# Running 26 expert tiles inside the attention steps of a fused expert–attention–expert block, and routing the second expert network earlier

## The reference

```
x = x + 0.5 * ffn(layernorm(x))      # "first network"
x = x + attention(layernorm(x))
x = x + 0.5 * ffn(layernorm(x))      # "second network", the same weights
# ffn: scores = softmax(x @ gate.T); the top 2 of 8 experts by scores + bias;
#      every routed row is scaled by its score, then
#      h = silu(row @ w1[e]) * (row @ w3[e]); out = h @ w2[e]   (128 -> 352 -> 128)
# attention: 16 heads of 8, softmax over 256 keys, output projection
```

## Time and profile before

| | |
|---|---|
| time, median of 3 runs | 758.16 us (757.82 to 762.54) |
| span of the profiled execution | 758.1 us, 14824 instructions |
| TensorE busy by its records | 618.2 us, 82% of the span |
| TensorE weight loads | 468.5 us, 62% |
| VectorE busy | 444.4 us, 59% |
| ScalarE busy | 388.9 us, 51% |
| GpSimd busy | 303.9 us, 40% |
| mean granted TensorE clock | 0.943 of full speed |

### The profile page before, as it was taken

How to read it: one execution, slowest core, us unless ns; L and a number is a source line. 1 busy time by engine, 2 the same in 40 slices (tenths; PEclk the granted TensorE clock), 3 DMA queues, 4 the chain that set the end, 5 groups by cost and what they waited for, 6 DMA issues and landing times.

```text
span 758.1 us, 14824 instructions
## 1 busy us (share of the span) xinstructions
PE 618.2 (82%) x5002; PEld 468.5 (62%) x5002; DVE 444.4 (59%) x1163; ACT 388.9 (51%) x910; POOL 303.9 (40%) x313
## 2 busy tenths in 40 slices
PE   5248999999979769899999998885999989999200
PEld 5237998999857334455554554454889979989200
DVE  4845652225346688989999999981567422233111
ACT  0524665444422456777777777773356544444000
POOL 6057533665423255014200010003475137777574
PEclk9999999999999788999999999997999999999755
DMA  7255888887982444345533444016479778887332
GB/s 255 70 182 158 237 237 224 228 239 211 265 262 75 128 130 136 101 133 157 160 101 101 148 127 120 3 44 206 128 194 244 240 191 232 263 236 229 112 80 62
DMA packets 116298, 126.02 MB, mean 166 GB/s; under 512 B 12480, under 2 KB 99008, under 8 KB 115968
## 3 DMA queue, kind: packets, MB, share of 16 engines
q1 hardware_dynamic: 98256, 100.15, 44.2%
q0 software_dynamic: 9088, 18.63, 9.9%
q10 hardware_dynamic: 8880, 6.30, 2.5%
HBM read 89.37 MB, written 35.39 MB: 165 GB/s over the span
## 4 chain that ended last, share of the span: by engine, by line
PE 53%; DVE 23%; DMA 7%; issue 6%; POOL 5%; ACT 4%; SPq 2%; POOLq 0%; ACTq 0%; DVEq 0%
PE banks L677 12%; DVE mx L809 10%; PE banks L649 9%; PE banks L658 8%; PE banks L665 8%; POOL rows L583 4%; PE banks L1061 4%; PE banks L467 2%; PE banks L639 2%; DMA xe<-routed_rows,idx 2%; PE banks L945 2%; PE banks L1034 1%; DMA X<-in_x 1%; DVE resid L796 1%; ACT PT L1075 1%
## 5 line engine op out<-in xcount | busy, mean ns | idle before, releaser
L563 POOL DMA_INDIRECT xe<-routed_rows,idx x156 | 151.4, 971 | 240.4 <-DMA routed_rows<-xn 102.6
L809 DVE TENSOR_REDUCE mx<-banks 128x2 f32<-128x512 f32 x256 | 163.2, 683 | 7.9 <-PE banks L1036 6.6
L1075 ACT ACTIVATE PT<-banks 128x512 f32<-128x512 f32 x256 | 140.6, 604 | 36.7 <-PE banks L1047 34.4
L583 POOL DMA_INDIRECT rows<-slots_out,slot x128 | 124.3, 971 | 71.1 <-issue 28.7
L730 DVE TENSOR_TENSOR hidT<-banks,act 96x256 f32<-96x256 f32 (+1 forms) x92 | 34.9, 380 | 197.2 <-ACT act L711 194.3
L677 PE MATMUL banks<-WR,hidT 128*128 128x128 f32 x936 | 119.8, 275 | 0.6 <-ACT ye L720 0.6
L677 PEld LDWEIGHTS banks<-WR,hidT 128*128 128x128 f32 x936 | 111.9, 191 | 3.0 <-issue 1.0
L649 PE MATMUL banks<-xeT,WR 128*128 128x256 f32 (+1 forms) x368 | 88.8, 365 | 7.6 <-DMA WR<-in_experts 3.4
L658 PE MATMUL banks<-xeT,WR 128*96 128x256 f32 (+1 forms) x368 | 84.7, 353 | 0.3 <-DVE hidT L730 0.3
L665 PE MATMUL banks<-xeT,WR 128*128 128x256 f32 (+1 forms) x368 | 82.8, 347 | 0.0
L1034 PE MATMUL banks<-KS,QS 56*128 56x256 bf16 x256 | 69.1, 286 | 12.2 <-DVE mx L809 10.5
(11 more groups left out here) (158 smaller groups left out, 870.3 us busy)
## 6 DMA issues: line engine op xcount, KB each, us to landing
WR<-in_experts SPq DMA_DIRECT2D x92, 544.0 KB
stacks<-split SPq DMA_DIRECT2D x32, 384.0 KB
slots_out<-ye SPq DMA_DIRECT2D x156, 64.0 KB
QS<-stacks SPq DMA_DIRECT2D x64, 112.0 KB
KS<-stacks SPq DMA_DIRECT2D x64, 112.0 KB
routed_rows<-xn ACTq DMA_DIRECT2D x16, 256.0 KB, 6.1
routed_rows<-xn SPq DMA_DIRECT2D x12, 256.0 KB, 2.3
xe<-routed_rows,idx POOLq DMA_INDIRECT x156, 4.7
```

The source lines that it names most:

```text
L563: eng.indirect_dma_start(xe[:, i % XR, a, :], None, routed_rows[h], bass.IndirectOffsetOnAxis(ap=idx[h][:, tile:tile + 1], axis=0))\
L583: eng.indirect_dma_start(rows[:, k, t, :], None, slots_out[h], bass.IndirectOffsetOnAxis(ap=slot[h][:, k, t:t + 1], axis=0))\
L809: eng.tensor_reduce(mx[:, :, e, pair], maxima_bank(f)[:, :].rearrange("p (q n) -> p q n", q=2), AX.X, ALU.max).then_inc(s_max, 1)
L1075: eng.activation(PT[:, u % 4, 1 - k].rearrange("p t n -> p (t n)"), PS[f % 3], ACT.Exp, scale=scale).then_inc(s_exp2, 1)
```

## The change

Loads 38 to 52 (`I0` to `I1`) leave the expert stages. They are 14 tiles of the first network (38 to 45) and 12 of the second (46 to 52). Each is computed as single tiles inside attention, one tile in two steps, a piece in each half step (`beat`): TensorE's pieces are gate columns, the previous tile's down product, value columns, the next tile's turn. Such a tile uses two banks of its own: `E1` (bank 2) holds gate columns and turned rows, `E2` (bank 7) holds value columns and the result. While they run, scores have banks 0 and 1 and maxima 3 and 4; between steps 17 and 84 (maxima) or 102 (scores) the third bank is back. Silu is taken as 0.5 z (1 + tanh(z / 2)): ScalarE does tanh, VectorE two `scalar_tensor_tensor`.

Attention now begins at step -13 (13 steps ahead of step 0 instead of 8) and holds batch 0's maxima there. The first 14 tiles run from step -13, the other 12 from step 104. Routing g = 2 is moved to steps 58 to 100, right behind batch 7. Half of its rows, and now half of g = 3's, are scaled by VectorE (`rows_vector`). `keep_pace` is gone. Routing g = 3 gets tables of its own counted from load 53, with three ticks of statistics inside attention. SyncE's weight fetches, result stores and row stores are placed in attention by due steps (`joint_due`, `until`). GpSimd's waits follow (`turned`).

The core of the diff, with what the next sections speak of:

```diff
+I0 = NL + 15
+I1 = HALVES * NL + 7
+STEP1 = -13
+STEP2 = 104
+WIDE_FROM = 17
+WIDE_MAX = 84
+WIDE_SCORE = 102
...
+def bank_turns(step_of, two, three, last_wide):
+
+    turns, held = [], {}
+    for f in range(BATCH * HEADS):
+        ring = three if WIDE_FROM <= step_of(f) < last_wide else two
+        bank = min(ring, key=lambda b: held.get(b, -1))
+        turns.append((bank, held.get(bank, -1) + 1))
+        held[bank] = f
+    return turns, held
+
+
+MAXIMA, MAXIMA_END = bank_turns(lambda f: f // 2 + STEP1, (3, 4), (3, 4, 7), WIDE_MAX)
+SCORES, SCORES_END = bank_turns(lambda f: f // 2, (0, 1), (0, 1, 2), WIDE_SCORE)
...
+        def rows_vector(eng, g):
+
+            eng.wait_ge(s_coef, 2 * (g + 1))
             eng.wait_ge(s_comb, GC * HALVES)
+            h = g % HALVES
             for t in range(TH):
-                eng.tensor_scalar(rows[:, 1, t, :], X[:, t, :], factor[:, 1, t:t + 1], offset[:, 1, t:t + 1],
+                if t % 4 == 0:
+                    eng.wait_ge(s_xn[t // 4], 16 * TOP_K * g)
+                eng.tensor_scalar(rows[:, 1, t, :], X[:, h * TH + t, :], factor[:, 1, t:t + 1], offset[:, 1, t:t + 1],
                                   ALU.mult, ALU.add).then_inc(s_xv, 1)
...
+        def rows_sync(eng, g):
+
+            for c in range(RG):
+                if g == 2:
+                    eng.wait_ge(s_xr, rows_made(g) + 4 * c + 4)
                     rows_store(eng, 0, 4 * c + 3, xn)
-                else:
-                    eng.wait_ge(s_xv, 4 * c + 4)
-                    rows_store(eng, 0, TH + 4 * c + 3, rows[:, 1])
+                eng.wait_ge(s_xv, TH * (g - 2) + 4 * c + 4)
...
+        def load_sync(eng, i, first, last):
+
+            if i < last:
+                weights(eng, i)
+            if i >= first + RING:
+                rows_out(eng, i - RING)
...
+        def joint_sync(eng, begin, end, first, last):
+
+            for i in range(begin, end):
+                load_sync(eng, i, first, last)
+                yield
+
+        def joint_due(begin, first, start, early):
+
+            def due(step):
+                n = 0
+                for i in range(begin, I1 + RING):
+                    tile = tiles_before(i - RING + 1) - tiles_before(first)
+                    ready = early if i < first + RING else start + (4 * tile + 2) // 2 + 1
+                    n += ready <= step
+                return n
+            return due
...
+            def turn(i, a, t):
+                if a == 0:
+                    eng.wait_ge(s_xe[i % XR], landed(i))
+                if t == J1:
+                    eng.wait_ge(s_exp2, SCORES_END[2] + 1)
+                wait(eng, s_jgate, t)
+                eng.transpose(E1[:, HC * P:], xe[:, i % XR, a, :], ident).then_inc(s_jxt, 1)
+
+            def up(i, a, t, bank, column):
+                for c in range(HC):
+                    k = P if c < HC - 1 else HT
+                    first = column + c * P
+                    done = eng.matmul(bank[0:k, c * P:(c + 1) * P], WR[:, i % WRING, first:first + k],
+                                      xeT[:, t % 2, 0:P], start=True, stop=True)
+                return done
+
+            def up_gate(i, a, t):
+                if a == 0:
+                    eng.wait_ge(s_wl[i % WRING], 16 * (i // WRING + 1))
+                eng.wait_ge(s_jxte, t + 1)
+                up(i, a, t, E1, 0).then_inc(s_ju1, 1)
+
+            def up_value(i, a, t):
+                if t == 0:
+                    eng.wait_ge(s_ve, 2)
+                if t == J1:
+                    eng.wait_ge(s_lgread, 2 * 3)
+                wait(eng, s_jye, t)
+                up(i, a, t, E2, HIDDEN).then_inc(s_ju3, 1)
+
+            def down(i, a, t):
+                eng.wait_ge(s_jhid, t + 1)
+                for c in range(HC):
+                    k = P if c < HC - 1 else HT
+                    done = eng.matmul(E2[:, HC * P:], hidT[0:k, t % 2, c * P:(c + 1) * P],
+                                      WR[0:k, i % WRING, 2 * HIDDEN + c * D:2 * HIDDEN + (c + 1) * D],
+                                      start=c == 0, stop=c == HC - 1)
+                done.then_inc(s_jy, 1)
+
+            tiles = joint_tiles(first, last)
+            turn(*tiles[0])
+            for j, tile in enumerate(tiles):
+                up_gate(*tile)
+                yield
+                if j > 0:
+                    down(*tiles[j - 1])
+                yield
+                up_value(*tile)
+                yield
+                if j + 1 < len(tiles):
+                    turn(*tiles[j + 1])
+                yield
+            yield
+            down(*tiles[-1])
+            yield
+
...
+            def copy_x(i, a, t):
+                eng.wait_ge(s_jxt, t + 1)
+                wait(eng, s_ju3, t - 1)
+                if t == 0:
+                    eng.wait_ge(s_u3, I0)
+                eng.copy(xeT[:, t % 2, 0:P], E1[:, HC * P:]).then_inc(s_jxte, 1)
+
+            def gate(i, a, t):
+                eng.wait_ge(s_ju1, t + 1)
+                wait(eng, s_jhid, t - 1)
+                if t == 0:
+                    eng.wait_ge(s_hid, I0)
+                eng.activation(act1[:, t % 2, 0:HC * P], E1[:, 0:HC * P], ACT.Tanh, scale=0.5).then_inc(s_jtanh, 1)
+
+            def copy_y(i, a, t):
+                eng.wait_ge(s_jy, t + 1)
+                if a == 0:
+                    wait(eng, s_st[i % RING], stored(i - RING))
+                eng.copy(ye[:, i % RING, a, :], E2[:, HC * P:]).then_inc(s_jye, 1)
...
+            for j, tile in enumerate(tiles):
+                yield
+                gate(*tile)
+                yield
+                if j > 0:
+                    copy_y(*tiles[j - 1])
+                yield
+                yield
+                yield
+                if j + 1 < len(tiles):
+                    copy_x(*tiles[j + 1])
+                yield
+                yield
+                yield
...
+            for i, a, t in joint_tiles(first, last):
+                yield
+                yield
+                eng.wait_ge(s_jtanh, t + 1)
+                eng.scalar_tensor_tensor(act1[:, t % 2, 0:HC * P], act1[:, t % 2, 0:HC * P], 1.0, E1[:, 0:HC * P],
+                                         ALU.add, ALU.mult).then_inc(s_jgate, 1)
+                yield
+                eng.wait_ge(s_ju3, t + 1)
+                eng.wait_ge(s_jgate, t + 1)
+                wait(eng, s_jy, t - 1)
+                if t == 0:
+                    eng.wait_ge(s_y, I0)
+                eng.scalar_tensor_tensor(hidT[:, t % 2, 0:HC * P], act1[:, t % 2, 0:HC * P], 0.5, E2[:, 0:HC * P],
+                                         ALU.mult, ALU.mult).then_inc(s_jhid, 1)
+                yield
+
+        def beat(streams, step):
+
+            for start, stream in streams:
+                if step >= start:
+                    next(stream, None)
...
-        def keep_pace(eng, products):
-
-            for _ in range(products):
-                eng.matmul(PS[4][:, 0:D], ident, WO[:], start=True, stop=True)
+        def steps():
+
+            for step in range(STEP1, PAIRS * BATCH):
+                n, u = divmod(step, PAIRS)
+                yield step, n, u, (2 <= n + 3 < BATCH, 0 <= n + 1 < BATCH, 0 <= n < BATCH, 0 <= n - 1 < BATCH)
...
+                for k in range(2):
+                    largest = largest_scores(eng, maxima_of(n, u), k)
+                    scores = head_scores(eng, n, u, k) if now else iter(())
+                    for _ in range(2):
+                        next(largest, None)
+                        next(scores, None)
...
+                if u % 2 == 0 and u > 0 and now:
+                    values(eng, n, u // 2 - 1)
+                if u == 0 and done:
+                    values(eng, n - 1, PAIRS // 2 - 1)
+                if u == 0 and n >= 2:
+                    turn_raw(eng, n - 2)
+                if ahead and u == 0:
+                    m = n + 3
...
-        def attention_scalar(eng, side, ticks):
...
+        def attention_scalar(eng, streams, side, ticks):
+            for step, n, u, (ahead, nxt, now, done) in steps():
...
+                for k in range(2):
+                    beat(streams, step)
                     if now:
-                        wait(eng, s_av, PAIRS // 2 * n + u // 2 - 1)
-                        for k in range(2):
-                            f = 2 * (PAIRS * n + u) + k
-                            eng.wait_ge(s_sc, f + 1)
-                            eng.activation(PT[:, u % 4, 1 - k].rearrange("p t n -> p (t n)"), PS[f % 3], ACT.Exp,
-                                           scale=scale).then_inc(s_exp2, 1)
...
+        def attention_sync(eng, *sides):
+
+            def until(step, counts):
+                for i, (side, due) in enumerate(sides):
+                    for _ in range(due(step) - counts[i]):
+                        next(side, None)
+                    counts[i] = max(counts[i], due(step))
...
+            for n in range(-2, BATCH):
                 if 2 <= n + 2 < BATCH:
```

(47 more changed lines are left out.)

484 lines of the change are left out of this document (239 added, 245 removed).

## The result

The changed kernel takes **794.33 us** (median of 4 runs, 792.74 to 797.79) against 757.99 beside it: ratio 1.0493 [1.0438, 1.0548], 36 us slower where 19 us faster were forecast. Its profiled execution spans 791.3 us. Times of runs are medians; of e8 and e10 the profiled execution was over 1.5% slower than the fastest of its kernel, and their ratios leave it out. The windows of the changed kernel are cut where the first scores of step 0 (243.5), step 16 (295.0) and step 104 (504.7) start, 0.5 us ahead of the exponentials at which the earlier trace rows cuts steps 16 and 104.

The account below looks back on a forecast made before the run. Attention was taken as bound by VectorE, 94% busy, with about 0.55 us of TensorE free per step. Against 758.1 us, -22.5 + 6.8 + 25 - 26.5 - 2 = -19.2 gave 739 us, range 729 to 750.

Parts of the forecast that it names:

- Part 1: Cost of one joint tile inside attention: 5.55 us per tile, 2.8 a step, with 2.5 as the floor.
- The loop that I drew round VectorE: In full joint steps, the next tile's turn waits for VectorE's first operation, queued behind a maximum: 5.55 us per tile.
- Lockstep: Rival for joint steps: each half step ends on a round trip, 3.5 us a step, +35, 774 us; chance 0.09.
- theory B: Follow-up theory for joint steps: each is a chain of round trips between TensorE, VectorE and ScalarE.
- Parts 2 and 3: Part 2: steps -13 to -1 take 33 us, gain 22.5; Part 3: steps 0 to 15 take 45, loss 6.8.
- Part 4: Routing g = 2 in steps 81 to 100, where nothing hides VectorE's work: +25 us (19 to 30).
- Part 5: Step 104 to load 53: 64 us (56 to 75) instead of 90.3, a gain of 26.5.
- Part 6: From load 53 on: 2 us gained (-3 to +3) from load 69's wait; last gathers unchanged.

Follow-up runs that it names:

- e8: e3 with four unread products in each of steps 84 to 100 to keep TensorE at work, and two score banks from step 80: 779.54 us.
- e10: e3 with the 32 inversion products of g = 2 spread over steps 97 to 100, and VectorE's end of the routing two steps later: 774.49 us.
- e12: Changed kernel with both halves' scores side by side and single joint pieces, one behind the scores, one at the step's end: 769.07 us.
- e13: Changed kernel with joint pieces two at a time behind the first half's scores, halves still apart: 802.17 us.
- e3: Changed kernel with TensorE's joint pieces two at a time behind the second half's scores, both halves side by side: 773.49 us.
- e4: Changed kernel with VectorE's and ScalarE's joint work on 8 columns instead of 384, rest of the gate left out, all waits kept: 789.39 us.
- e1: Changed kernel without any joint tile, loads 38 to 52 run as ordinary loads, routing of g = 2 still in steps 81 to 100: 797.28 us.
- e7: Kernel before plus first network's joint tiles with paired pieces; `finish` chunk of step -13 a step later, that of steps 25 to 37 spread: 756.67 us.
- e9: e3 with both `finish` chunks shifted as in e7, and VectorE's half of routing g = 3's rows back on ScalarE: 782.00 us.
- e5: Changed kernel with only the first network's joint tiles; routing g = 2, second network and routing g = 3 as in the kernel before: 768.06 us.
- e2: Changed kernel with only the first network's 14 joint tiles; the second network's loads all run behind attention: 790.38 us.
- e11: e7 with only the first network's last 7 tiles joint, one in four steps, the other 7 alone ahead of attention: 771.59 us.

## Why the prediction was wrong

**Part 1 (the joint tile) was mis-sized by what stands between the halves.** The sum took a half of scores at 0.23 from the earlier trace rows and up and down at 0.67, each from a place where products of the same layout follow. (the earlier trace rows shows the scores for the maxima, beside which the other scores run.) In the change a piece on 128 rows stands behind every half: a half takes 0.32, a piece 0.86. That is 4 x 0.09 + 3 x 0.19 = 0.9 us a tile that the forecast had at nothing. e12 brings the 93.4 ahead of step 16 down to 82.4 and the 77.4 behind step 104 to 66.7: 21.7 of the 30 us by which these three stages missed, or 0.8 a tile; behind step 104 that is, by the estimate at e13, 0.58 for the halves and 0.31 for waits on copies and on VectorE, which the other order shortened as well. The start of step 16 says the same in every run of the 13 steps with 14 joint tiles: 295.5 to 303.7 in five kernels with the halves parted, 283.7 to 291.5 in six paired ones, 282.5 to 285.9 in three of e12's order. How it comes about stands in e3's timeline:

```profile
551.97 0.29 PE L1257 MATMUL banks<-QS,KS 58*128 58x256 bf16 x2
552.09 0.28 PE L1259 MATMUL banks<-QS,KS 58*128 58x256 bf16 x2
552.30 0.93 PE L847 MATMUL banks<-xeT,WR 128*128 128x128 f32 x6
```

Side by side, the first products of both halves count as one group at 551.97, the second ones at 552.09, and the piece starts at 552.30: 0.33 for two, as much as for one alone. The code puts the halves into different rows (`ROWS * e`), 58 of 128 each. The Trainium skill, "TensorE: Matmul & The Clock Gate", section "Part 3: Packing small matmuls — row/col tiling", says that products in different row groups run at once. The trace agrees: two halves in 0.33. A joint piece uses all 128 rows; its first product starts 0.20 behind the last of the half ahead, and the next half's first 0.20 behind the last of the piece. So a tile's piece between the halves buys the second half's full price. With maxima in the step a half is a pair in itself, and steps 104 to 111 gained 0.36 each all the same (3.24 to 2.88 in e12); there the runs don't part the halves from the smaller number of changes of kind.

The loop that I drew round VectorE, the other half of Part 1, was no bound at all: e4 took 0.8 us a tile out of VectorE, half of it out of the loop, and step 104 to load 53 did not move. Nor was Lockstep the reason: it is a chain of round trips, theory B, which e3 and e4 exclude; that its bound of 0.5 us a joint step was nearly reached (3.2 against 2.8 in steps 0 to 15) is chance.

**Parts 2 and 3.** With the halves side by side (e12), steps -13 to 15 take 82.4 (78 forecast): cut at 235, where step 0's scores start, 33.4 for the 33 (VectorE busy for 27.5 of them, where 28.4 were forecast) and 49.0 for the 45. So Part 2 was right but for the price of the halves, and the 4 left over lie in steps 0 to 15, at a granted clock of 0.93; what holds them no run tells. In the change itself the stand of 2.92 us and the 1.2 GHz behind it come on top.

**Part 4 (routing in steps 81 to 100): +25 forecast, +37 measured.** The mechanism was right: nothing hides VectorE's work there. In steps 80 to 103 VectorE is busy for 43.4 of 46.0 us in the kernel before and for 65.0 of 76.1 in e1: 21.6 more work, where I had 20.7. What I mis-sized is its idle time, 11 us instead of 2.6. 7.4 of it lie in the eight steps of the inversion (second row of e3). The forecast had put the 32 inversions on TensorE at nothing and the waits for them at 1 us; in the change's trace they are two blocks of 2.5 us (485.55 and 491.76), and behind them VectorE waits 1.41 and 3.49 us for scores whose maxima it is to take. This is read from the trace: neither a high clock (e8) nor a spread inversion (e10, inconclusive) gave the idle time back, and what would is open. Another 5.7 us came in steps 24 to 39, where the forecast expected nothing: e7 showed that these come from where `finish` stands there.

**Part 5.** Its miss of 15 is Part 1's price for 10.7 of it. And what the stage did gain was never the joint tiles': e1 has 75.4 without them, where the kernel before has 88.2 between the same events. What left the stage with the routing is its VectorE work and the wait of 7.68 for the gather; the forecast gave one gain of 26.5 for the move and the tiles together, and so never asked what the tiles alone would bring.

**Part 6: -2 forecast, +8 measured** (6.7 from load 53's turn, 208.6 against 201.9), and as much without any joint tile (e1: 208.7, with the list of routing g = 3 seven loads earlier). 5.3 of it lie in loads 60 to 69. TensorE stands 2.82 at 614.87 for VectorE's row sums, where the kernel before has no such stand. Routing g = 3 has the same list in 14 loads instead of 18, and I had priced only the gather at its end, which did improve (load 69 waits for nothing). e9 excludes the rows as the cause; that it is the closer list as such is argued, not shown.

**The balance of the routing's move** the forecast never drew by itself: it has +25 in Part 4 against shares of -26.5 and -2. e5 beside e2 gives 22 us of loss. The move took the routing out of a stage where VectorE was busy for 41 of 49 us, with a stand of TensorE behind it, and put it into steps 80 to 103, where VectorE was busy for 94%.

## What to carry to other kernels

Price a piece of work by what it interrupts: a duration read where like follows like is a lower bound, and small products that share the array in different rows lose that when something else is put between them. Moving work into a stage whose engine is 94% busy costs at least its full length (here 21.6 us of work cost 30); ask first which engine the move relieves, and draw the balance of each move by itself. Then check the order of the first idea before giving it up: with the halves kept together and the routing left where it was, the first network's 14 joint tiles made a kernel 1% faster.

## What the runs showed of the hardware

Two halves of scores in different rows take 0.33 us together and 0.32 alone. Where the rows or columns of the array that a product uses change (58 and 128 rows, 128 and 32 columns), TensorE needs 0.20 us to the first start instead of 0.11, and 0.21 more to a piece's second product; another type or another line on the same 128 rows costs nothing of the kind (0.11 to 0.13). A stand of 2.92 us was followed by 18 us at 1.2 GHz (granted clock 0.50), though TensorE was busy in all of them; and steps 0 to 15 ran at 0.85 with the thinner work of e11, at 1.00 with that of e7. Raising the clock from 0.85 to 1.00 in steps 80 to 95 (e8) left their time as it was, 49.4 and 49.0 us, where VectorE was 93% busy.
